# ScalarE reordered around the attention's two absolute-maximum halves, eight early roundings, and the second product's offsets written into PSUM by ScalarE

## The reference, cut to what matters

```python
def reference(x, ctx_1024, ...):                       # x: (4, 2048, 512), ctx: (4, 154, 512), fp32
    x = x + xattn(layernorm(x), ctx, ctx, Wq, bq, Wk, bk, Wv, bv, Wo, bo)   # 16 heads of 32, causal mask over 154 keys
    x = x + ffn(layernorm(x), w1, conv_w, conv_b, w2)                       # 512 -> 2048 -> 512
    return x

def ffn(x, w1, conv_w, conv_b, w2):
    h = einsum(act_quant(x), weight_quant(w1))         # 8-bit rows, ternary weights
    h = silu(depthwise_conv1d(h, conv_w, conv_b))      # three taps along the sequence
    return einsum(act_quant(h), weight_quant(w2))      # rows rounded to 8 bits by their absolute maximum
```

## Time and profile before

| | |
|---|---|
| median of 3 runs | 1622.62 us (1622.56 to 1625.26) |
| profiled execution, its time | 1627.43 us |
| profiled execution, its span | 1625.6 us |
| PE busy | 1502.7 us (92%), 9149 matmuls |
| DVE busy | 1348.6 us (83%) |
| ACT busy | 1105.7 us (68%) |
| POOL busy | 1027.6 us (63%) |
| mean DMA rate | 52 GB/s |

### The profile page before, as it was taken

The page is one execution under the profiler, slowest core; times in us unless marked ns, Lnnn a source line. Parts: engine busy times, 40 slices in busy tenths (PEclk is TensorE's granted clock), DMA queues, the critical chain, the costliest instruction groups (busy, mean ns, idle before and its releaser), DMA issues.

```text
span 1625.6 us, 24734 instructions
## 1 busy us (share of the span) xinstructions
PE 1502.7 (92%) x9149; PEld 902.7 (56%) x9149; DVE 1348.6 (83%) x2078; ACT 1105.7 (68%) x1976; POOL 1027.6 (63%) x838
## 2 busy tenths in 40 slices
PE   9799898999999999999999999999999999998875
PEld 6376454747465555647464655647474655555322
DVE  7566797798879888898879798888979898878897
ACT  3447486949587785949496776849395877858462
POOL 4101375867666786867666767858666767768452
PEclk8979799999999999999999999999999999999987
DMA  8540202021220303021310303031210202020000
GB/s 259 137 137 27 66 7 66 7 53 47 51 65 8 92 7 92 8 67 40 69 40 7 92 7 92 7 96 20 60 40 20 80 8 65 8 66 1 29 26 27
DMA packets 80342, 85.20 MB, mean 52 GB/s; under 512 B 29983, under 2 KB 55839, under 8 KB 79709
## 3 DMA queue, kind: packets, MB, share of 16 engines
q1 hardware_dynamic: 80221, 83.62, 18.9%
HBM read 38.74 MB, written 19.42 MB: 36 GB/s over the span
## 4 chain that ended last, share of the span: by engine, by line
PE 61%; ACT 22%; DVE 13%; issue 3%; POOL 1%; DMA 0%; DVEq 0%; ACTq 0%; SPq 0%
PE ps L1041 12%; PE ps L857 12%; PE ps L955 10%; PE ps L863 9%; ACT hqb L1160 5%; ACT h L1263 4%; PE ps L974 4%; DVE pm L1643 4%; ACT h L1258 3%; ACT pexp L1239 3%; PE ps L826 3%; PE ps L675 2%; DVE h L1634 2%; ACT hl L1160 2%; PE ps L1023 1%
## 5 line engine op out<-in xcount | busy, mean ns | idle before, releaser
L640 POOL TENSOR_TENSOR h<-h,gall 128x512 f32<-128x512 f32 x235 | 339.7, 1445 | 18.4
L650 POOL TENSOR_TENSOR h<-h,r 128x512 f32<-128x512 f32 x240 | 306.3, 1320 | 67.0 <-DVE qb L1754 41.3
L638 POOL TENSOR_TENSOR gall<-gall,cw 128x512 f32<-128x512 f32 x235 | 257.6, 1096 | 135.4 <-DVE h L1634 135.4
L1634 DVE SCALAR_TENSOR_TENSOR h<-gall,cw,h 128x512 f32<-128x512 f32 x256 | 259.9, 1017 | 83.5 <-ACT h L1258 83.3
L857 PEld LDWEIGHTS ps<-va,pexp 128*128 128x128 f32 x2048 | 266.5, 197 | 29.1 <-issue 9.8
L1160 ACT ACTIVATE hqb<-h 128x512 f16<-128x512 f32 x276 | 172.3, 683 | 148.0 <-PE ps L1041 142.8
L863 PE MATMUL ps<-xqT,w1T 128*128 128x512 f16 x1024 | 258.3, 383 | 10.3 <-DVE gall L1559 7.4
L857 PE MATMUL ps<-va,pexp 128*128 128x33 f32 x2048 | 264.3, 274 | 0.0
L1559 DVE SCALAR_TENSOR_TENSOR gall<-ps,bias,srow 128x512 f32<-128x512 f32 x256 | 191.1, 747 | 73.2 <-PE ps L863 43.8
L1041 PE MATMUL ps<-w2T,hqb 128*128 128x512 fp8e4 x960 | 244.6, 382 | 0.0
L1258 ACT ACTIVATE h<-gall,cb,cw 128x512 f32<-128x512 f32 x256 | 221.8, 866 | 8.5
(11 more groups left out here) (219 smaller groups left out, 2317.9 us busy)
## 6 DMA issues: line engine op xcount, KB each, us to landing
qs<-hl SPq DMA_DIRECT2D x192, 128.0 KB, 2.6
xr<-in_x SPq DMA_DIRECT2D x16, 1024.0 KB, 5.5
out<-xr SPq DMA_DIRECT2D x64, 256.0 KB
h<-in_L_ffn_w SPq DMA_DIRECT2D x8, 1024.0 KB, 5.6
srow<-in_L_xattn_bo SPq DMA_DIRECT2D x15, 256.0 KB, 3.2
kst<-kh_scratch SPq DMA_DIRECT2D x32, 38.5 KB
xr<-in_ctx SPq DMA_DIRECT2D x1, 1024.0 KB
h<-in_L_xattn_Wk SPq DMA_DIRECT2D x1, 1024.0 KB, 8.4
```

Of the source, the lines that this page charges most:

```text
L638: gp.tensor_tensor(right, right, cw[:, c, 2:3].to_broadcast([P, TB]), ALU.mult).then_inc(c2m_ok, 1)
L640: gp.tensor_tensor(hc(c), hc(c), right, ALU.add).then_inc(c2p_ok, 1)
L650: gp.tensor_tensor(hc(c), hc(c), r2[:], ALU.mult).then_inc(u_ok, 1)
L1634: ve.scalar_tensor_tensor(out=hc(c), in0=g[:, c % 4, 1:TB + 1], scalar=cw[:, c, 1:2], in1=hc(c), op0=ALU.mult, op1=ALU.add).then_inc(c1_ok, 1)
```

## The change

Five edits, all in the steady slots.

1. The matmul that writes the offset is gone from `mm2` in the slots of `late_results`; the first product matmul has start=False. ACT writes -1536 times `csum2` into the bank with a copy, `offset(i)`: 0 and 1 behind `centre(0)` and `centre(1)`, 2 behind `centre(3)`, 3 behind the quantising of the rows. `csum2` is therefore made 128 rows high, once, in slot 1.
2. `mm2(1)` moves ahead of `spread_scales`.
3. Eight roundings instead of four stand at the end of slots 1 to 14, and in the steady slots `rounded(c)` waits only for `mm2(3)` to have passed channel tile c (a new semaphore, yq_ok), not for all of y_ok.
4. On ACT `at_high` moves ahead of `silu` 8 to 12.
5. On DVE `absmax(0)` moves behind `at_low`, as it already stood in slot 15.

```diff
-        csum2 = sb("csum2", [1, D], F16)
+        csum2 = sb("csum2", [P, D], F16)
...
-        EARLY = 4
+        def early(s):
+
+            return 8 if s < NB - 1 else 4
...
-                r = mm(F[1][0:1, :], onesh[:, 0:1], w2T[:, c, :], start=c == 0, stop=c == CT - 1)
+                r = mm(F[1], onesh[:, 0:P], w2T[:, c, :], start=c == 0, stop=c == CT - 1)
...
                     if cs[0] == 0:
                         if i == 0:
                             pe.wait_ge(hq_ok, at(s, CT, -CT))
-                        if do_a and s != NB - 1:
-                            if i < 3:
-                                pe.wait_ge(x2_ok, at(s, TT, (1, 2, 4)[i]))
-                            else:
-                                pe.wait_ge(out_ok, at(s, 4, 2 - 8))
-                        elif s == NB and i >= 2:
-                            pe.wait_ge(out_ok, at(s, 4, i - 1 - 8))
-                        mm(bank, negh[0:1, :], csum2[:], start=True, stop=False)
+                        if late_results(s):
+                            pe.wait_ge(of_ok, at(s - 2, TT, i + 1))
+                        else:
+                            if s == NB and i >= 2:
+                                pe.wait_ge(out_ok, at(s, 4, i - 1 - 8))
+                            mm(bank, negh[0:1, :], csum2[0:1, :], start=True, stop=False)
                     for c in cs:
-                        r = mm(bank, hq(c)[:, i * P:(i + 1) * P], w2T[:, c, :], start=False, stop=c == CT - 1)
+                        r = mm(bank, hq(c)[:, i * P:(i + 1) * P], w2T[:, c, :], start=False, stop=c == CT - 1,
+                               skip_group_check=late_results(s))
                     if cs[-1] == CT - 1:
                         r.then_inc(y_ok, 1)
+                    elif i == 3 and late_results(s):
+                        r.then_inc(yq_ok, 1)
...
                 if do_a and do_m:
                     mm2(0)
+                    mm2(1)
...
                 if do_a and do_m:
-                    mm2(1)
                     mm2(2, range(0, 8))
...
                 def rounded(c):
-                    if c == 0 and do_m:
+                    if late_results(s):
+                        act.wait_ge(yq_ok, at(s - 2, 8, c // 2 + 1))
+                    elif c == 0 and do_m:
                         act.wait_ge(y_ok, at(s, TT, -TT))
...
+                def offset(i):
+
+                    if i < 3:
+                        act.wait_ge(x2_ok, at(s, TT, (1, 2, 4)[i]))
+                    else:
+                        act.wait_ge(out_ok, at(s, 4, 2 - 8))
+                    copy(ybank(s, i), csum2[:], scale=-HALF).then_inc(of_ok, 1)
...
-                    if do_f and do_a and c > LASTU:
+                    if do_f and do_a and LASTU < c < CT:
                         for k in SILUS[c - LASTU - 1]:
                             silu(k)
...
-                if do_f:
-                    for k in range(SILUS[-1].start if do_a else CT - 3, CT - 3):
-                        silu(k)
...
-                    for k in range(CT - 3, CT):
+                    for k in range(SILUS[CT - LASTU - 1].start if do_a else CT - 3, CT):
                         silu(k)
...
                     if do_a:
                         centre(i)
+                    if late_results(s) and i != 2:
+                        offset((0, 1, 2, 2)[i])
...
+                if late_results(s):
+                    offset(3)
                 if do_f and s != NB - 1:
-                    for c in range(EARLY if do_a else CT):
+                    for c in range(early(s) if do_a else CT):
                         rounded(c)
...
-                if do_f and do_a and s != NB - 1:
-                    absmax(0)
...
-                if s == NB - 1:
+                if do_f and do_a:
                     absmax(0)
-                if do_f and do_a:
                     absmax(1)
```

More of the change, by code:

```diff
@@ L349, in build @@
         y_ok = sem("y_ok")
+        of_ok = sem("of_ok")
+        yq_ok = sem("yq_ok")
         out_ok = sem("out_ok")
@@ L907, in fix_mm2 @@
                     pe.wait_ge(fx_act, 5)
-                    mm(A[2][0:NF, :], negh[0:1, 0:NF], csum2[:], start=True, stop=False)
+                    mm(A[2][0:NF, :], negh[0:1, 0:NF], csum2[0:1, :], start=True, stop=False)
                     for c in range(CT):
@@ L1135, in slot @@
                     for i in range(TT):
-                        mm(ybank(s, i), negh[0:1, :], csum2[:], start=True, stop=False)
+                        mm(ybank(s, i), negh[0:1, :], csum2[0:1, :], start=True, stop=False)
                     for c in range(CT):
@@ L1352, in slot @@
                     if do_m and s != NB + 1:
-                        for k in range(EARLY + 2 * c, min(EARLY + 2 * c + 2, CT)):
+                        for k in range(early(s - 1) + 2 * c, min(early(s - 1) + 2 * c + 2, CT)):
                             rounded_late(k)
@@ L1417, in slot @@
                     act.wait_ge(w_cs, 2)
-                    copy(csum2[:], F[1][0:1, :]).then_inc(csum_ok, 1)
+                    copy(csum2[:], F[1]).then_inc(csum_ok, 1)
                 if do_q:
@@ L1436, in slot @@
                 if s == NB - 1:
-                    for c in range(EARLY):
+                    for c in range(early(s)):
                         rounded(c)
```

## The result

| | before | changed kernel | ratio, 95% interval |
|---|---|---|---|
| median (lowest to highest) | 1622.59 us (1622.4 to 1625.26) | 1605.72 us (1600.79 to 1611.1), 4 runs | 0.9879 [0.9845, 0.9914] |
| profiled execution | 1627.43 us | 1609.67 us, span 1607.9 | |
| measured again, on another occasion | 1623.26 us | 1601.62 us (1598.07 to 1606.76), 6 runs | 0.9859 [0.9833, 0.9885] |

The account below looks back on a forecast made before the run. The prediction saw no engine full: an 89.4 us slot bound by a relay among engines. Ten plain slots (17.5 us), three masked-query slots (6.9) and slot 15 (1.1) made 25.5 off 1622.6: 1597.1 us, range 1590 to 1611.

Parts of the forecast that it names:

- The halves: Edits 4 and 5: PE's 1.92 us wait moves from ahead of project_out to ahead of turn_pm, at 2.1; worth 0.
- so I take the whole clock: Step assuming that PE's clock stays full behind the 2.1 us wait ahead of turn_pm.
- rival A: PE's clock falls behind the wait ahead of turn_pm, stretching product matmuls, 1.15 to 1.2 us in every slot; chance 0.08.
- The offsets: Four offset matmuls leave PE, so DVE's last maximum ends 1.05 us earlier per slot; ACT's 0.60 us copies cost 0.
- spread_scales behind mm2(1): spread_scales ends 3 us later, POOL starts at 710.55 instead of 708.63; what queues behind on ACT still finishes in time.
- Eight early roundings: At the slot's end mm1 starts 1.3 us behind the last maximum instead of 1.99: another 0.7 us per slot.
- rival B: Early roundings wait for slower POOL tiles and delay negmT; at 1.63 us a tile 1.1 us lost, 1611; chance 0.07.
- The sum: Plain slots gain 1.75 us each, masked-query slots 2.3 each, slot 15 1.1; together 25.5 us.
- C: Clock stays low through both products ahead of spread_scales; just past the point 1625 to 1635, all 32 at half 1682; chance 0.05.
- D: Only DVE's 1.05 us pass, since something unseen holds mm1 at 1.99 behind the last maximum: 1606; chance 0.06.
- E: Offset copies or roundings wait in a ring with DVE, so the slot keeps 89.4 us: 1622; chance 0.04.
- The last slot's 1.1: In slot 15 at_low no longer waits 1.13 us for ACT behind five silu: 1.1 us gained.

Follow-up runs that it names:

- e4_no_halves: The changed kernel with at_high and absmax(0) put back where they were (edits 4 and 5 undone): median 1592.5 us, ratio 0.9811.
- e13_spread_late: e4_no_halves with the first half of mm2(2) ahead of spread_scales as well: median 1606.7 us, ratio 0.9896 against the kernel before.
- e5_spread_first: The changed kernel with mm2(1) again behind spread_scales (edit 2 undone): median 1594.5 us, ratio 0.9823.
- e6_mm2_ahead: The changed kernel with mm2(0) ahead of turn_pm in the steady slots: median 1595.1 us, ratio 0.9814.
- e7_fill: The changed kernel with eight constant matmuls of 512 columns in PE's wait behind project_out: median 1595.7 us, ratio 0.9827.
- e11_slot0_fill: The kernel before with edits 1 and 3 alone, plus two wide constant matmuls ahead of each of scores 2 to 9 in slot 0: median 1592.0 us, ratio 0.9801.

## Why the prediction was right, and where not

*The halves, worth 0.* Right for the relay: the wait moved as described, to 2.1 us. The step that failed is "so I take the whole clock", with the chance of 0.08 for rival A. The clock fell in 6 of the 13 slots (5 in the second profile). A fall cost 0.96 us in a plain slot (88.32 against 87.36) and 1.6 in one with masked queries (90.3 against 88.75 in e4_no_halves), where A had 1.15 to 1.2 in every slot. Nothing of it shows in the slot behind. Together the falls took 7.8 us in the first profile and 7.0 in the second, which is the whole distance to e4_no_halves and more than the 3.7 us that slots 2 to 14 missed. A fall in each slot, by the rule that the prediction quotes from the Trainium skill (TensorE: Matmul & The Clock Gate, "HAM oscillation"), is not what the trace shows either, with 6 and 5 of 13; that section tells it of a kernel with longer waits.

*The offsets, 1.05.* Measured alone: 1.21. The copy from SBUF to PSUM, taken as 0.60, took 0.58 to 0.62 and cost nothing.

*spread_scales behind mm2(1), taken as free.* With the full clock no slot shows a price for it. But the text overlooked two things behind it. It has `offset(3)` used by the transposes at 722, while mm2(3) needs it, 0.9 us behind its end; e13_spread_late uses this room up. And POOL's last tile now lies beside a small operation of DVE, which is held but takes nothing from the slot. What edit 2 is worth by itself is not settled: undone in the changed kernel it takes the falls away (the sum falls by 7.5 to 8.3 us), undone in e4_no_halves it leaves six slots in which DVE's last tap is held (the sum rises by 4.8 us).

*Eight early roundings, 0.7.* Right: 0.79, mm1 1.20 us behind the last maximum. POOL had 0.47 us to spare where the text had 0.6, and rival B, off at eight, is real at twelve.

*The sum.* Plain slots with the full clock gained 2.0 (forecast 1.75), those with masked queries 2.7 (91.43 to 88.75 in e4_no_halves; forecast 2.3). For slots 2 to 14 the text had 24.4 us; without the reordering they give 28.5, with it 20.7 to 21.5. Rivals C and D did not occur, E neither. (The slack of 0.85 us in C is 0.55 by the text's own 711.9 and 712.45, and the 32 matmuls that it puts at 6.92 us took 7.07; the forecast does not hang on either.) The last slot's 1.1 can't be told from what the clock does there (176.7 to 178.6 us for the rest behind slot 14 in most kernels).

*The median.* 1597 was forecast, 1605.7 and 1601.6 were measured, inside 1590 to 1611. The direction and the terms of the slot held; what was mis-sized is the price of the moved wait, forecast 0, measured 7 to 8. That the median lies as near to the forecast as it does is in part luck, since the other terms gave 4.1 us more than forecast. Slot 0, which the text did not look at, took 100.7 and 87.7 us in two executions of the changed kernel.

A version without the reordering does better: e4_no_halves has a median of 1592.5 us, and five of its six runs are faster than all six of the changed kernel beside them, though the two intervals touch. e5_spread_first, e6_mm2_ahead, e7_fill and e11_slot0_fill lie within 3.2 us of it, and their intervals overlap.

## What to carry to other kernels

Moving a wait of PE from one place to another in a relay is not free even where nothing waits for either place: look at how long PE then pauses and what it must do next, and count a fall of the clock there by the matmuls behind it and by whoever they delay in the same slot. When a step is moved later, follow every engine that it starts through all that is queued behind it, and ask who waits for each piece: here a copy of ACT, two pieces behind, was what PE came to wait for. An operation that takes longer than before is not yet a price: here one of DVE's was held for up to 1.5 us beside POOL's tiles, and the slot took it back. So add up where the slot grew before naming a cause. Compare kernels by the stretches that the change touches: a start-up stretch with its own clock can move the whole time by more than the change.

## What the runs showed of the hardware

- A copy of 128x512 from SBUF (f16) into a PSUM bank on ACT takes 0.58 to 0.62 us, like one out of it.
- DVE's TENSOR_SCALAR on 128x4 numbers in SBUF was held until POOL's run of tiles was over, up to 1.51 us in e13_spread_late, longer than one tile (20.09 / 16 = 1.256 us): between two tiles it did not get in. BATCH_NORM_STATS2 (0.68 us) and the maxima, which read PSUM (0.716 us), were not held beside the same tiles.
- Where DVE's tap and POOL's operation, both on SBUF, are recorded as starting within 0.12 us of each other, the one or the other is held until the other is done. In the slots looked at DVE got through from a lead of 0.054 us on and was held at 0.048 and less. It makes a slot 1.1 us longer or not, from slot to slot of one program.
- Waits of PE of 2.09 to 2.86 us ahead of four transposes and the fp8 products were followed by a fall of the clock in 15 of 28 slots, waits of 1.77 to 1.80 us there in 1 of 13, and waits of 1.86 to 1.94 us ahead of 48 f16 matmuls in none of 38. Behind a fall 16 products of 128x512 took 5.31 us instead of 3.63, and 32 took 8.76 instead of 7.07.
- PE stayed at 1.2 GHz from 95 to 133 us in e6_mm2_ahead though it was never idle, with matmuls of 33 to 154 columns between single ones of 512. With two more of 512 ahead of each of eight scores the slot took 87.4 us; the same code without them took 87.7 us once, so the one profile does not show that the fillers did it.
